# Attention layer of a four-stage transformer stack: how the first batch is opened, and how rows are normalized and biased

## What is computed

```python
x = x + tanh(g_xattn[0]) * L0_xattn(layernorm(x), ...)        # quantized linears
x = x + tanh(g_ffn[0])   * L0_ffn(layernorm(x), ...)          # 8 experts, top 2, plus one shared expert
x = x + tanh(g_xattn[1]) * L1_xattn(layernorm(x), ctx, ...)   # this stage
x = x + tanh(g_ffn[1])   * L1_ffn(layernorm(x), ...)          # 8 experts, top 2

# L1_xattn: 32 heads of 16, 4 batches of 512 rows
q = rope(x @ Wq); k, v = split(ctx @ Wkv); k = rope(k)
w = softmax(q @ k.T / 4)
out = (w @ v) @ Wout + bout
```

## Time and profile before

| what | value |
|---|---|
| median of 3 runs | 1326.58 us (1325.49 to 1328.86) |
| the profiled execution's own time | 1326.52 us |
| its span, first to last instruction | 1324.8 us |
| PE busy | 1166.8 us, 88% |
| DVE busy | 831.1 us, 63% |
| ACT busy | 666.2 us, 50% |
| POOL busy | 396.0 us, 30% |
| mean granted TensorE clock | 0.960 of full speed |

### The profile page before, as it was taken

How to read it: one execution, slowest core, us unless ns; L and a number is a source line. 1 busy time by engine, 2 the same in 40 slices (tenths; PEclk the granted TensorE clock), 3 DMA queues, 4 the chain that set the end, 5 groups by cost and what they waited for, 6 DMA issues and landing times.

```text
span 1324.8 us, 16521 instructions
## 1 busy us (share of the span) xinstructions
PE 1166.8 (88%) x5247; PEld 512.9 (39%) x5309; DVE 831.1 (63%) x1283; ACT 666.2 (50%) x1175; POOL 396.0 (30%) x469
## 2 busy tenths in 40 slices
PE   5877776899999999859799989999999999889997
PEld 4544443565444444423232223222322222234543
DVE  6798765234555554146988887778777777624543
ACT  2565554565222222236366666566656656662453
POOL 4566531002322222042324422222222233101332
PEclk8888898999999999978899999999999999999999
DMA  7324125654544444194325433222222235200011
GB/s 252 114 104 135 56 88 182 234 181 163 201 144 141 145 154 131 56 308 107 111 73 140 118 103 93 70 85 78 68 89 80 79 84 65 40 1 9 33 40 49
DMA packets 111029, 145.79 MB, mean 110 GB/s; under 512 B 24952, under 2 KB 79736, under 8 KB 110440
## 3 DMA queue, kind: packets, MB, share of 16 engines
q1 hardware_dynamic: 91816, 113.47, 26.5%
q0 software_dynamic: 18368, 28.85, 8.5%
q10 hardware_dynamic: 768, 2.49, 0.5%
HBM read 99.54 MB, written 48.37 MB: 112 GB/s over the span
## 4 chain that ended last, share of the span: by engine, by line
PE 30%; DVE 12%; issue 7%; ACT 6%; DMA 1%; POOL 1%; ACTq 0%; POOLq 0%; DVEq 0%
PE PS L2887 7%; DVE a_top L3214 5%; PE PS L2853 5%; PE PS L2788 5%; PE PS L2872 4%; PE PS L2812 3%; PE PS L2391 2%; ACT shared_w L3009 2%; PE PS L2414 1%; ACT a_E L3009 1%; DMA a_attnT<-f_y,l_pos 1%; DVE a_mcut L3134 1%; POOL a_K L2151 1%; PE PS L2800 1%; DVE a_early L3094 1%
## 5 line engine op out<-in xcount | busy, mean ns | idle before, releaser
L3214 DVE TENSOR_REDUCE a_top<-PS 128x2 f32<-128x1024 f32 x256 | 308.7, 1222 | 88.3 <-PE PS L2872 84.4
L3009 ACT ACTIVATE shared_w<-PS 128x512 f32<-128x512 f32 x256 | 138.8, 596 | 78.4 <-PE PS L2853 78.4
L2853 PE MATMUL PS<-a_Q,a_K 99*128 99x512 bf16 (+1 forms) x468 | 156.8, 388 | 17.7 <-ACT a_E L3009 4.2
L3009 ACT ACTIVATE a_E<-PS 128x512 f32<-128x512 f32 x256 | 139.0, 597 | 64.6 <-PE PS L2853 64.5
L1502 PE MATMUL PS<-f_W,f_GT 128*128 x312 | 141.4, 596 | 0.0
L2872 PE MATMUL PS<-a_K,a_Q 64*128 64x512 bf16 x512 | 100.5, 389 | 15.6 <-DVE a_top L3214 9.4
L2853 PEld LDWEIGHTS PS<-a_Q,a_K 99*128 99x128 bf16 (+1 forms) x512 | 44.6, 98 | 153.7 <-ACT shared_w L3009 51.1
L1931 POOL TENSOR_TENSOR a_qf<-a_qf,a_tab 128x512 f32<-128x512 f32 x15 | 19.0, 1268 | 284.3 <-DVE a_swapped L3116 284.3
L1558 DVE TENSOR_TENSOR f_H<-f_SG,PS 128x256 f32<-128x256 f32 x39 | 16.4, 421 | 115.1 <-ACT f_SG L1542 115.1
L1502 PEld LDWEIGHTS PS<-f_W,f_GT 128*128 128x128 f32 x312 | 56.7, 192 | 57.3 <-issue 57.3
L2788 PE MATMUL PS<-a_xT,a_early 128*128 128x512 f32 x128 | 72.3, 662 | 2.1 <-ACT a_xT L2975 0.7
(11 more groups left out here) (381 smaller groups left out, 2088.1 us busy)
## 6 DMA issues: line engine op xcount, KB each, us to landing
f0r_raw<-in_L_ffn_W_dram SPq DMA_DIRECT2D x24, 512.0 KB, 4.6
a_K<-k_parts SPq DMA_DIRECT2D x192, 64.0 KB, 2.3
a_Q<-a_q_parts SPq DMA_DIRECT2D x186, 64.0 KB, 2.5
f_y<-f_Y SPq DMA_DIRECT2D x39, 256.0 KB, 2.0
v_units<-V SPq DMA_DIRECT2D x16, 512.0 KB, 2.9
a_V<-v_units SPq DMA_DIRECT2D x16, 512.0 KB, 3.4
k_parts<-f_k_parts SPq DMA_DIRECT2D x16, 384.0 KB, 3.5
a_q_parts<-a_parts SPq DMA_DIRECT2D x16, 384.0 KB, 2.8
```

Source lines behind the costliest of these rows:

```text
L2853: nc.tensor.matmul(PS[:, 4 + h % 2, :], K6[k][0:rows_, o, head // 2, kt * P:(kt + 1) * P], Q6[k][0:rows_, o, head // 2, :], start=True, st ...
L3009: nc.scalar.activation(E[step % 2][:, h, :], PS[:, 4 + h % 2, :], ACT.Exp).then_inc(exp_done, 1)
L3214: nc.vector.tensor_reduce(top[:, h - h % 2:h - h % 2 + 2, t], PS[:, 2 * pair:2 * pair + 2, :], AX.X, ALU.max).then_inc(maxed, 1)
```

## The change

The first row fetches get a fourth buffer, so all four tiles of batch 0 are requested at once. DVE takes each tile's statistics right behind its addition and normalizes batch 0 ahead of the turns. SP issues Wq only when tile 0 is added, and bias, table, K and V only when three tiles are; the bias is first of these, and the second shared-expert load goes between the K and V of units (0, 0) and (0, 1). The shared-expert loads are cut in four. Transposes of batch 0 alternate between banks 7 and 3. The u of late tile 2 is halved, and LATE is laid out anew. Batch 1 is measured in slots 8 to 13 of turn (-1, 3), its root comes after slot 14, and it is normalized in slots 4 to 7 and biased in 8 to 11 of turn (0, 0), a tile a slot; its transposes go to slots 10, 12, 13, 14. Batches 2 and 3 are normalized in slots 8 to 11 and biased in 12 to 15, a tile a slot. Tiles 8 to 15 are added one turn later. In turns (1, 3) and (3, 2) the four p parts stand together in slot 6 and 12.

```diff
 class LateTiles:
-    DOWN = (6, 0, 1, 2, 6, 6, 6, 6)
+    DOWN = (6, 0, 1, 6, 6, 6, 6, 6)
     def load(self, sp, k):
-        sp.dma_start(self.homes[k], self.xT_dram[k]).then_inc(self.loaded[k], 16)
+        for c in range(self.DC):
+            sp.dma_start(self.homes[k][:, c, :], self.xT_dram[k][:, c, :]).then_inc(self.loaded[k][c], 16)
...
-        rows = Combine(nc, sb, sem, X, F32, weights, pos, ffn_gate, ys, 3, [attnT[1][:, d, :] for d in range(DC)])
+        rows = Combine(nc, sb, sem, X, F32, weights, pos, ffn_gate, ys, 4, [attnT[1][:, d, :] for d in range(DC)])
...
+            beside_root = {(1, DC - 1): 6, (NB - 1, 2): 12}.get((b, c))
-            add(5 if crowded else 6, "a", before(b, c, 1))
+            add(5 if crowded else 8 if beside_root == 6 else 6, "a", before(b, c, 1))
...
-                for d, when in enumerate((6, 7, 8, 10)):
+                for d, when in enumerate((10, 12, 13, 14) if b == 0 else (6, 7, 8, 10)):
...
-            for d, when in enumerate((13, 14, 15, 15) if crowded else (12, 13, 14, 15)):
+            for d, when in enumerate([beside_root] * DC if beside_root else (13, 14, 15, 15) if crowded else (12, 13, 14, 15)):
...
-        LATE = {(-1, 0): {9: [("g", 2, 0), ("y", 0, 0), ("y", 1, 0), ("t", 2, 0)]},
-                (-1, 2): {4: downs(2) + ups(3), 5: [("g", 3, 0), ("y", 2, 0)] + ups(4), 6: [("t", 3, 0), ("g", 4, 0)] + downs(3),
-                          7: [("y", 3, 0), ("t", 4, 0)], 8: downs(4, [0]), 9: downs(4, [1]), 10: [("y", 4, 0)] + ups(5, [0]), 11: ups(5, [1]),
-                          12: ups(5, [2]), 13: ups(5, [3]), 14: [("g", 5, 0)], 15: [("t", 5, 0)]},
+        LATE = {(-1, 0): {9: [("y", 0, 0), ("y", 1, 0)]},
+                (-1, 2): {4: ups(2, [2, 3]) + ups(3), 5: [("g", 2, 0), ("t", 2, 0)] + downs(2), 7: [("y", 2, 0), ("g", 3, 0)],
+                          8: [("t", 3, 0)] + ups(4, [0]), 9: downs(3), 10: ups(4, [1]), 11: [("y", 3, 0)] + ups(4, [2]),
+                          12: ups(4, [3]), 13: [("g", 4, 0)] + ups(5, [0]), 14: [("t", 4, 0)] + ups(5, [1]), 15: ups(5, [2])},
...
+            if kind == "x" and unit[0] == 0:
+                return PS[:, (7, 3)[extra % 2], :]
...
             late.load(sp, 0)
+            sp.wait_ge(rows.tile_added, 1)
             sp.dma_start(wq, Wq.rearrange("(c p) n -> p c n", p=P)).then_inc(wq_loaded, 16)
...
+                    else:
+                        sp.wait_ge(rows.tile_added, TB - 1)
+                        sp.dma_start(tbias[:], bout.partition_broadcast(P)).then_inc(tbias_loaded, 16)
                     sp.dma_start(tab[0][:], tables_dram[bass.ds(unit[0], 1)].rearrange("a p k s -> p (a k) s")).then_inc(tab_loaded, 16)
...
                     load_kv(unit)
+                    late.load(sp, 1)
                     load_kv((0, 1))
...
-                if is_first(unit):
-                    sp.dma_start(tbias[:], bout.partition_broadcast(P)).then_inc(tbias_loaded, 16)
-                    late.load(sp, 1)
...
                     if is_first(unit) and h == 0:
-                        pe.wait_ge(late.added, 3 + pair)
+                        pe.wait_ge(late.added, 3)
...
+            def first_tile(t):
+                rows.vector(v, t)
+                v.wait_ge(rows.tile_added, t + 1)
+                first_norm.step(nc.vector.bn_stats(stats[:, t, :], X[:, t, :]))
             rows.vector_start(v)
-            rows.vector(v, 0)
+            first_tile(0)
+            first_tile(1)
             late.gate(v, 0)
-            rows.vector(v, 1)
+            first_tile(2)
             late.gate(v, 1)
-            rows.vector(v, 2)
-            rows.vector(v, 3)
+            first_tile(3)
...
+            v.wait_ge(sd_ready, 1)
...
+                last = nc.vector.tensor_scalar(xh[:, t, :], X[:, t, :], mv[:, t, 0:1], rstd[:, t:t + 1], ALU.subtract, ALU.mult)
+            last.then_inc(xh_ready, 1)
...
-                    at(4, aggregate)
-                    at(8, normalize)
-                    at(12, add_bias)
+                    pieces = [[t] for t in range(TB)] if nb else [list(range(TB))]
+                    for i, tiles in enumerate(pieces):
+                        if nb:
+                            at((8 if nb > 1 else 4) + i, lambda tiles=tiles: normalize(tiles))
+                        at((12 if nb != 1 else 8) + i, lambda tiles=tiles: add_bias(tiles))
```

More of the change, by code:

```diff
@@ L2608, in bank_of @@
         def bank_of(kind, unit, extra):
-            return PS[:, (7, 4, 5, 6)[extra[0]], :] if kind == "p" and unit[0] == NB - 1 else PS[:, 7, :]
+            if kind == "p" and unit[0] == NB - 1:
+                return PS[:, (7, 4, 5, 6)[extra[0]], :]
+            if kind == "x" and unit[0] == 0:
+                return PS[:, (7, 3)[extra % 2], :]
+            return PS[:, 7, :]
         def n_unit(unit, per=1):
@@ L2635, in batch_to_norm, with batch_to_measure @@
         def batch_to_norm(b, c):
-            nb = {0: b + 1 if b == -1 else None, DC - 1: b + 2}.get(c)
+            nb = {0: b + 1 if b < 1 else None, DC - 1: b + 2 if b >= 0 else None}.get(c)
             return nb if nb is not None and is_batch(nb) else None
+        def batch_to_measure(b, c):
+            if (b, c) == (0, 0):
+                return None
+            return 1 if (b, c) == (-1, DC - 1) else batch_to_norm(b, c)
+        MEASURE_AT = {1: (8, 13)}
         def tiles_to_add(b, c):
-            if b == -1 and c < 2 or b == 0:
-                first = TB + 2 * c if b == -1 else 2 * TB + 2 * c
+            turn_ = DC * b + c
+            if -DC <= turn_ < 2 - DC or 0 < turn_ <= DC:
+                first = TB + 2 * c if b == -1 else 2 * TB + 2 * (turn_ - 1)
                 return [first, first + 1]
@@ L2915, in _ @@
             late.down(pe, 1, 1)
-            for c in range(DC):
+            for c in range(2):
                 late.up(pe, 2, c)
@@ L2945, in _ @@
             late.take(act, 1)
-            late.silu(act, 2)
             def turn(b, c):
@@ L3009, in exps, with root @@
                         nc.scalar.activation(E[step % 2][:, h, :], PS[:, 4 + h % 2, :], ACT.Exp).then_inc(exp_done, 1)
+                def root(nb):
+                    act.wait_ge(var_ready, nb + 1)
+                    nc.scalar.activation(sd[:], mv[:, :, 1], ACT.Sqrt, bias=ln_eps[:]).then_inc(sd_ready, 1)
                 def take_sum(unit, g):
@@ L3020, in turn @@
                 for step in range(8):
-                    nb = batch_to_norm(b, c)
-                    if step == 3 and nb is not None:
-                        act.wait_ge(var_ready, nb + 1)
-                        nc.scalar.activation(sd[:], mv[:, :, 1], ACT.Sqrt, bias=ln_eps[:]).then_inc(sd_ready, 1)
+                    nb = batch_to_measure(b, c)
+                    if step == 3 and nb not in (None, 1):
+                        root(nb)
                     if (b, c, step) == (NB - 1, 2, 6):
@@ L3030, in turn @@
                     slot(2 * step)
+                    if step == 7 and nb == 1:
+                        root(1)
                     exps((b, c), step, (2, 3))
@@ L3066, in turn @@
                     at(10 + 4 * i, lambda t=t: add_rows(t))
-                nb = batch_to_norm(b, c)
-                if nb is not None:
-                    chn = Chain(v, steps_norm, nb * NORM)
+                measured = batch_to_measure(b, c)
+                if measured:
+                    chs = Chain(v, steps_norm, measured * NORM)
+                    first, collect = MEASURE_AT.get(measured, (0, 4))
                     for t in range(TB):
                         def stat(t=t):
-                            v.wait_ge(rows.tile_added, nb * TB + t + 1)
-                            if t == 0 and nb:
-                                v.wait_ge(sd_ready, nb)
-                            chn.step(nc.vector.bn_stats(stats[:, t, :], X[:, bass.ds(nb * TB + t, 1), :].rearrange("p a d -> p (a d)")))
-                        at(t, stat)
+                            v.wait_ge(rows.tile_added, measured * TB + t + 1)
+                            if t == 0:
+                                v.wait_ge(sd_ready, measured)
+                            chs.step(nc.vector.bn_stats(stats[:, t, :], X[:, bass.ds(measured * TB + t, 1), :].rearrange("p a d -> p (a d)")))
+                        at(first + t, stat)
                     def aggregate():
-                        chn.wait()
+                        chs.wait()
                         v.nop(nofuse=True)
```

71 lines of the change are left out of this document (45 added, 26 removed).

## The result

The changed kernel took 1318.49 us (median of 6 runs, 1316.11 to 1320.85), the kernel before on the same chip 1325.95: a ratio of 0.9946, 95% interval 0.9931 to 0.9962. So it is faster by 7.5 us, not by 17.9, and lies outside the range of 1303 to 1316.

A forecast was written before the change was run, and what follows sets the result against it. It took PE to bound the steady turns, with three longer root turns and the opening unproductive. 12.4 + 0.5 - 1.0 - 0.2 + 1.0 + 2.9 + 2.3 = 17.9 us gave 1308.6, range 1303 to 1316.

The forecast's parts named there:

- Step 6: Turns: (0, 0) loses 1 us, (1, 0) 0.2; (0, 3) gains 1.0, (1, 3) 2.9, (3, 2) 2.3.
- Step 4: Opening, q's reload to first maxima: 8.1 us before, plus one hop; maxima at 609.9, a gain of 12.4 us.
- Step 3: SP's queue in the opening: SP free at 597.5 and the opening's bound; store lands in 3.5 us, reload at 601.0.
- the backlog argument: Opening: 6.3 MB, 21 us at 297 GB/s, stands behind the rows, so q's store lands in 3.5 us, not 2.54.
- Steps 1, 2 and 5: Opening: transposes start at 583.5, q ends at 590.7; from maxima to exponentials, 46.5 us before, 0.5 us gained.
- rival D: Slower: late tiles 3 to 7 share bank 6; maxima to exponentials 75 us instead of 46.5, total 1337; chance 0.04.
- My own signs of being wrong: First exponential after 662, or the three root turns (0, 3), (1, 3) and (3, 2) keeping their lengths.
- Rival C: The turns give nothing, as the low clock comes elsewhere in them: 6.2 us less gain, 1315; chance 0.10.
- A: Opening: row fetches aren't faster, or delayed loads return the gain; rows at 581.5, slow K, later store, 1315; chance 0.18.
- B: Opening: PE pauses for normalization, clock 0.50 for transposes and projection, 4.4 us; total 1312; chance 0.10.
- E: Opening: pieces of the cut load don't overlap, 7.6 us on SP's path instead of 1.2; total 1315; chance 0.03.

The follow-up runs named there:

- e7: Changed kernel, but in turn (0, 0) batch 1 normalized in slots 0 to 3, biased in 12 to 15, transposes in 6, 7, 8, 10: 1310.1 us.
- e10: e7, but batch 1's transposes stay in slots 10, 12, 13, 14 as in the changed kernel: 1311.9 us.
- e2: Changed kernel with batch 1 (statistics, root, normalization, bias, transposes) and row additions as in the kernel before: 1311.5 us.
- e3: Changed kernel, but ACT issues its half of q's reload, and one constant fill, behind the silus of late tiles 2 and 3: 1314.3 us.
- e12: e11 with K and V of unit (0, 1) issued behind the store and reload of the first q: 1307.3 us.
- e11: e7 with ACT's half of q's reload behind the silus of tiles 2 and 3 and the copy of tile 2's transposes: 1308.6 us.
- e1: Kernel before with only the turns' part: batches 2 and 3 a tile a slot, p parts together in turns (1, 3) and (3, 2): 1316.9 us.
- e6: e5 with K and V of unit (0, 1) issued behind the store and reload of the first q: 1308.2 us.
- e5: Changed kernel with the edits of e2 and e3 together: 1309.4 us.
- e9: Changed kernel's opening and late-tile layout alone; batch 1, row additions, blocks of batches 2 and 3 and p parts as before: 1318.4 us.

## Why the prediction was wrong

**Step 6 failed, in turn (0, 0).** It said "PE will wait there: 1 us lost, bounds 0 and 3"; 7.6 us were lost. The reasoning was by totals: DVE would have 0.3 us more work, with 5.5 us free in the turn (30.25 less 24.76). The total was not the trouble (e7 has DVE busy 26.39, 1.6 more than before, and takes 31.73). DVE's timeline in the changed kernel shows what was:

```profile
679.27 0.53 DVE L3141 TENSOR_SCALAR a_early<-X,a_mv,a_rstd 128x512 f32<-128x512 f32 x1
679.72 1.26 DVE L3185 TENSOR_SCALAR a_ntop<-a_top 128x32 f32<-128x32 f32 x1
...
682.00 1.02 DVE L3193 TENSOR_TENSOR a_mcut<-a_ntop,a_mcut 128x32 bf16<-128x32 f32 x1
683.06 1.23 DVE L3267 TENSOR_REDUCE a_top<-PS 128x2 f32<-128x1024 f32 x1
```

Four normalizations and the pair swap stand ahead of a chain of five dependent steps that feeds PE two slots later. PE idles 2.0 us for it. The chain itself was slow, 3.3 us (679.72 to 683.02) against 2.4 in e7. At their shortest its steps take 0.2 us, but L3185 took 1.26 and L3193 1.02, and each ended within 0.05 us of the end of an instruction of POOL's on the next q (L1934 at 680.93, L1939 at 682.97); in e7 L3187 took 1.18 and ended with POOL's L1934 too. No run takes POOL's work away, so this share, 0.9 us, is read from the traces and not tested.

Two of batch 1's four transposes cost 1.8 and 0.8 more. Their late slots alone don't explain it, since e10 has them too and shows no wait. The first one, at 691.54, began as DVE finished with the bank that both use (L3209, until 691.48), and DVE had the last bias piece just ahead of that. And after the 2.0 us the clock is low: 0.50 from 684 to 686 and 0.70 to 688, full again by then; with the low stretch at the turn's start it runs at 0.93 over the turn, so some 5.3 of 37.87 us were at 1.2 GHz, an estimated 2.7 us lost. PE's listed waits are 5.3 us against 0.6 before, 4.7 more, and the two together are 7.4 of the 7.6. I had priced the first effect at 1 and named neither the second nor the third. Other slots for the same work give 6.1 us of the turn back (e7), and batch 1 treated as before gives 7.0 of the median (e2).

**Step 4 failed.** It took the old 8.1 us from reload to maxima and added one hop, 8.9; it was 10.9. The wait for q's store stands in ACT's queue, and before the change nothing that PE needed at once was behind it, as tile 2 had been through. The change put tile 2's silu behind it. I had followed the moved work on PE and on SP, and not asked what is queued behind ACT's wait. e3 shows this wait. The maxima came 5.4 us later than predicted: 2.0 by this step, 1.7 by the store's landing and 1.8 by its later issue.

**Step 3, a bound and a size.** SP was free at 594.0, not 597.5 (the bias took 0.34 us to issue, not 2.45, and the two K 12.7, not 14.4), and the store waited for DVE's cutting, not for SP. So SP was not the bound of the opening. The store then took 5.2 us to land where 3.5 were charged; e12 shows that K and V of (0, 1) in front of it are the cause, as the backlog argument had it.

**Steps 1, 2 and 5 held, 1 and 2 with 2.4 us missing.** Transposes at 584.99 (583.5 predicted), full clock through the projection, q done at 593.1 (590.7; the transposes took 4.4 us instead of 3.5). From maxima to exponential 46.0 us against 46.5, the 0.5 us gain predicted, though more late work was in it: rival D, slower, found no ground. That it matches so closely is luck: counted from DVE's first maximum the stretch was 45.9 us before and 45.3 here, and 43.9 to 45.7 in five other kernels with the same layout there (e3, e7, e10, e11, e12). At the maxima the gain was 7.0 instead of 12.4. My own signs of being wrong didn't fire: the exponential came before 662 and the three root turns got shorter. They left out turn (0, 0).

**The other turns.** (0, 3) gave 0.75 for 1.0, (1, 3) 1.7 for 2.9, (3, 2) 3.3 for 2.3: together 5.7 for 6.2. The last is outside its bound of 2.6, and (1, 3) runs at full clock now, with PE still waiting 1.3 us for DVE's maxima. That the sum fits is in part misses that cancel. Rival C is refuted by e1, whose three turns are as short.

**Rivals A, B and E.** The total came out 3.5 us above A's 1315, and turn (0, 0), which A doesn't have, is the reason. Of A's own terms the late rows came in part (tile 3's last rows were used at 580.4; 578.3 predicted, 581.5 in A), the longer landing of the store too, and the slow K did not. B's low clock didn't come in this profile, yet it did in e6 and e11. E's cost didn't come for the first load: its four pieces were issued in 1.75 us, PE started 3.1 us after the first issue (563.29 to 566.42) and ran all 16 u matmuls in one stretch of 9.46 us. In the kernel before PE started after 4.8 us (562.91 to 567.67), but there Wq, table, K and V were issued right behind the load, so this 1.7 us is not the cut's alone; no run has the cut by itself. The Trainium skill, "DMA: Bandwidth & Descriptors", section "Bandwidth", has the rule to batch DMAs to 1 MiB or more for bandwidth. Here the four pieces, which PE takes one by one, held nothing up. The fixed 2.0 us that step 3 took from the Trainium skill, "DMA: Bandwidth & Descriptors", section "Anatomy of one DMA", stands there for transfers issued by GpSimd, and these are SP's.

## What to carry to other kernels

When an edit moves work into another stretch, add up the queue, not the total: list what comes next on that engine and how soon another engine needs it, above all ahead of a chain of dependent small steps. For every wait in an in-order queue ask what the change has put behind it. Test a bundle of edits in parts: here two gained 6.6 and 9.1 us, the new slots of batch 1 gave 7 of them back, and the sum looked like a modest success.

## What the runs showed of the hardware that was not expected

Short idle times cost more than themselves. After 6.8 us of idle PE the next four d matmuls took 3.78 us instead of 1.98, and in turn (0, 0) an idle time of 2.0 us was followed by 2 us at 0.50 of the clock. But before the last projections nearly the same idle time, 1.04 us in the kernel before and 0.90 in the changed one, was followed by a clock of 0.53 in the first and 1.00 in the second. So whether the clock falls differs between executions of nearly the same work. That may be part of why the runs of one kernel lie 2 to 12 us apart; it was read from profiles and not tested by itself.

A store of 384 KB, issued about 35 us after the first row fetch, took 3.8 to 6.4 us to land behind 13 other transfers (the changed kernel, e2, e3, e5, e7, e9, e10) and 2.5 with these moved behind it (e12). Issued at 38 us it took 2.5 with them in front too (e11).

Small steps of DVE that take 0.2 us at their shortest took 1.0 to 1.3 beside an instruction of POOL, and ended with it (turn (0, 0) of the changed kernel and of e7). That was read from traces and not tested.
